# Sixteen weight low parts on VectorE and scatters alternating with scatter-adds in a one-core ViT tower kernel

## What is computed

```python
h = layernorm(einsum(layernorm(patches), W_proj) + b_proj)      # 576 tokens, 192 wide
h = h + attention(layernorm(h))                                 # 12 heads, q = cos(x) * cos(theta)
x = layernorm(h)
top_logits, top_idx = top_k(x @ router_w.T, 2)
top_w = softmax(top_logits)
for e in range(8):
    w_e = sum(top_w * (top_idx == e))
    hid = silu(x @ Wg[e].T) * (x @ Wu[e].T)
    out = out + hid @ Wd[e].T * w_e[:, None]
h = h + out
```

## Time and profile before

| What | Value |
|---|---|
| median of 3 runs | 224.12 us (221.51 to 225.14) |
| profiled execution: own time | 221.61 us |
| its span, first to last instruction | 219.8 us |
| mean granted TensorE clock | 0.959 of full speed |
| busy: TensorE, VectorE, ScalarE, GpSimd | 88%, 61%, 58%, 65% of the span |
| first expert step begins | 106.18 us |

### The profile page before, as it was taken

The page is one execution under the profiler, slowest core; times in us unless marked ns, Lnnn a source line. Parts: engine busy times, 40 slices in busy tenths (PEclk is TensorE's granted clock), DMA queues, the critical chain, the costliest instruction groups (busy, mean ns, idle before and its releaser), DMA issues.

```text
span 219.8 us, 4734 instructions
## 1 busy us (share of the span) xinstructions
PE 193.2 (88%) x1549; PEld 148.5 (68%) x1549; DVE 133.2 (61%) x418; ACT 127.7 (58%) x296; POOL 142.5 (65%) x190
## 2 busy tenths in 40 slices
PE   0599999999998879899999999995999986999950
PEld 0588999999996556473576777763676754677630
DVE  3789998369977846664733576865355441444420
ACT  0534468983598999899576667652344441344430
POOL 7699855599999724999895887785224322222222
PEclk9999999999999999976999999999699998899996
DMA  5999999689577731666676135444411223222111
GB/s 191 411 432 303 388 396 398 243 289 372 151 217 234 236 104 40 203 186 181 215 212 187 49 101 154 126 87 91 81 21 18 25 33 47 50 32 45 18 18 18
DMA packets 17152, 36.29 MB, mean 165 GB/s; under 512 B 2633, under 2 KB 7017, under 8 KB 16489
## 3 DMA queue, kind: packets, MB, share of 16 engines
q1 hardware_dynamic: 13753, 27.43, 39.1%
q0 software_dynamic: 2944, 2.76, 8.5%
q10 hardware_dynamic: 432, 5.80, 6.4%
HBM read 31.63 MB, written 4.36 MB: 164 GB/s over the span
## 4 chain that ended last, share of the span: by engine, by line
PE 59%; DMA 13%; POOL 8%; ACT 6%; issue 5%; DVE 4%; SPq 2%; POOLq 1%; ACTq 0%; DVEq 0%
PE ps L1249 19%; DMA experts<-x_t 7%; PE ps L1468 3%; PE ps L1473 3%; PE ps L1472 3%; PE ps L1470 3%; PE ps L1469 3%; PE ps L1480 3%; DMA out<-shared 3%; POOL slot_x L604 3%; PE ps L1228 2%; PE ps L1497 2%; PE ps L1496 2%; PE ps L1498 2%; ACT experts L702 2%
## 5 line engine op out<-in xcount | busy, mean ns | idle before, releaser
L413 POOL TENSOR_TENSOR experts<-stage,experts 128x528 bf16<-128x528 f32 x52 | 60.9, 1202 | 18.4 <-ACT experts L667 18.3
L1249 PE MATMUL ps<-experts 128*117 128x193 f32 (+1 forms) x320 | 55.9, 334 | 8.6 <-DVE experts L933 8.1
L1249 PEld LDWEIGHTS ps<-experts 128*117 128x117 f32 (+1 forms) x320 | 53.5, 185 | 9.5 <-DMA experts<-x_t 8.5
L1179 DVE TENSOR_TENSOR shared<-shared,ps 128x256 f32<-128x256 f32 x48 | 20.2, 421 | 46.7 <-ACT shared L834 46.7
L834 ACT ACTIVATE shared<-ps 128x256 f32<-128x256 f32 x48 | 18.5, 384 | 36.8 <-PE ps L1473 36.8
L667 ACT CAST experts<-stage 128x528 f16<-128x528 f32 x64 | 38.8, 631 | 1.0 <-DMA stage<-w_exp 1.0
L649 ACT ACTIVATE experts<-experts 128x468 f32<-128x468 f32 x40 | 22.7, 589 | 18.3 <-POOL experts L506 6.9
L618 POOL DMA_INDIRECT out<-shared x8 | 12.4, 1545 | 29.0 <-ACT shared L859 23.5
L1496 PE MATMUL ps<-experts,shared 128*128 128x192 f16 (+1 forms) x96 | 24.1, 251 | 1.6 <-DVE shared L1184 1.6
L1497 PE MATMUL ps<-experts,shared 128*128 128x192 bf16 (+1 forms) x96 | 24.1, 251 | 0.0
L1498 PE MATMUL ps<-experts,shared 128*128 128x192 f16 (+1 forms) x96 | 24.1, 251 | 0.0
(11 more groups left out here) (230 smaller groups left out, 340.3 us busy)
## 6 DMA issues: line engine op xcount, KB each, us to landing
stage<-w_exp SPq DMA_DIRECT2D x64, 264.0 KB, 3.1
experts<-x_t ACTq DMA_DIRECT2D x3, 1888.0 KB, 10.1
experts<-w_proj SPq DMA_DIRECT2D x4, 768.0 KB, 7.9
experts<-x_t SPq DMA_DIRECT2D x4, 472.0 KB, 8.6
experts<-x_t SPq DMA_DIRECT2D x1, 1888.0 KB, 15.1
slot_x<-experts SPq DMA_DIRECT2D x1, 1032.0 KB, 6.1
shared<-slot_x SPq DMA_DIRECT2D x8, 129.0 KB, 2.1
out<-h SPq DMA_DIRECT2D x1, 351.0 KB
```

The source lines that it names most:

```text
L413: ops.tensor_tensor(lo_w[:, to + EW:to + EW + PW], stage[:, n % STAGES, :], hi_w[:, to:to + PW], ALU.subtract).then_inc(split_pool if on_p ...
L1249: last = mm(dst, xbuf[:, t % 2, k, 0:m], gw[:, k, :], start=k == 0, stop=k == KT - 1)
```

## The change

Four edits. The low parts of pieces 48 to 51 go from GpSimd to VectorE, which now has sixteen, one in each of sixteen steps from 2 to 19; GpSimd has five behind the attention phase instead of nine. Scatters and add-outs alternate: two scatters, add-out 0, two scatters, add-out 1, and so on up to the tenth scatter, and then the other add-outs. ScalarE casts one piece more (46) ahead of the experts, so that every later cast comes a step earlier.

```diff
--- before.py
+++ after.py
@@ -59,7 +59,7 @@
     STAGES = 7
     GROUPS = [(0, 3), (3, 5)]
     GN = 3
-    POOL_FIRST = 52
+    POOL_FIRST = 48
     VEC_TILES = (1, 2, 4)
     EPS = 1e-5
     BIG = 512.0
@@ -73,8 +73,8 @@
-    VEC_PIECES = tuple(range(52, 64))
-    VEC_STEPS = (8, 9, 11, 12, 14, 15, 16, 17, 18, 19, 20)
+    VEC_PIECES = tuple(range(48, 64))
+    VEC_STEPS = (2, 3, 4, 5, 6, 8, 9, 11, 12, 13, 14, 15, 16, 17, 18, 19)
     def on_pool(n):
         return n not in VEC_PIECES
@@ -622,12 +622,11 @@
             pool.wait_ge(blank_out, 32)
             pool.wait_ge(xs_ready, len(GROUPS))
             pool.wait_ge(out_base, 32)
-            scatter_rows(0, 6)
-            add_out(0)
-            scatter_rows(6, 9)
-            add_out(1)
-            scatter_rows(9, 10)
-            for c in range(2, CHUNKS):
+            scatter_rows(0, 2)
+            for c in range(4):
+                add_out(c)
+                scatter_rows(2 + 2 * c, 4 + 2 * c)
+            for c in range(4, CHUNKS):
                 add_out(c)
         @block.scalar
@@ -825,7 +824,7 @@
                 last = a.activation(gexp[0:TOK, t:t + 1], top[0:TOK, t, 0:1], ACT.Exp, bias=top[0:TOK, t, 1:2], scale=-1.0)
             last.then_inc(gexp_ready, 1)
             load_table(ACT.Silu)
-            high_parts(44, 46)
+            high_parts(44, 47)
             def silu(n):
                 sc.wait_ge(gu_done, n + 1)
@@ -859,7 +858,7 @@
                 a.activation(yc[:, c % YB, :], pcol(Y_BANKS[c % 2], 0, D), ACT.Copy, scale=w).then_inc(y_ready, 1)
             rows_high(0)
-            high = 46
+            high = 47
             for n in range(NSTEP):
                 c, r = divmod(n, STEPS)
                 silu(n)
@@ -1212,9 +1211,7 @@
                 if r == 2 and 1 <= c <= E:
                     slot_facts(c - 1)
                 if n in VEC_STEPS:
-                    rests(52 + VEC_STEPS.index(n), 53 + VEC_STEPS.index(n))
-                if n == VEC_STEPS[-1]:
-                    rests(63, 64)
+                    rests(48 + VEC_STEPS.index(n), 49 + VEC_STEPS.index(n))
             hidden_low(NSTEP - 1)
         @block.tensor
```

## The result

The changed kernel takes 211.87 us (median of 4 executions, 211.42 to 212.41), the kernel before 223.56 (221.51 to 225.14, the three shown ahead of the prediction and one more). The ratio is 0.951 with a 95% interval of 0.943 to 0.958: faster. The prediction was 213.0 us in a range of 210.5 to 219.0.

The account below looks back on a forecast made before the run. TensorE was taken to bound the expert phase, losing time only in two holes: - 4.62 - 4.85 + 0.3 = - 9.2 us on the profiled 221.61 gives 212.4. Predicted 213.0 us, range 210.5 to 219.0.

Parts of the forecast that it names:

- Hole one: TensorE's 2.21 us wait before step 21 for piece 63, with slow clock behind it, goes: 4.62 us gained.
- Hole two: TensorE's 3.05 us wait in step 34 for chunk 12's rows, behind queued add-outs, goes with its slow clock: 4.85 us.
- The sum of holes: Both TensorE holes, before step 21 and in step 34, go whole in the full change: 9.47 us together.
- The last scatter: On GpSimd's alternating queue the last scatter is issued at 145.0 us, against 148.82 before.
- the slack in step 22: Chunk 8's rows arrive at 150.0 and TensorE wants them at 153.0: 3.0 us slack, so scatters stay hidden.
- rival one: Each VectorE low part costs a GpSimd scatter 0.70 us, the last slips 6.3 us, TensorE idles in step 22: 217.5 us; chance 0.12.
- Low parts against GpSimd's: VectorE's low parts in steps 2 and 3 wait 0.6 us each on GpSimd's; cost on the path 0, at most 0.2.
- Rival four: VectorE's low parts wait on GpSimd's, gate products come late, TensorE falls to 1.2 GHz: 224.9 us; chance 0.03.
- The port between VectorE and GpSimd: Nine low parts fall on scatters at 0.25 us each, 2.3 us, rather than 0.70 each, 6.3 us, by the exclusive lock.
- The cast: One more ScalarE cast ahead of the experts moves TensorE's first expert step back by 0.3 us, bounds 0 to 1.
- The signs: Among the signs of being right: each add-out from the fifth on waits for ScalarE's yield, not for a landing.
- 213.0 rather than 212.4: The sum gave 212.4 us from a fast profiled execution of 221.61; the median before was 224.12, so 213.0 was predicted.

Follow-up runs that it names:

- the run with the last two in step 20: Changed kernel with the low parts of pieces 62 and 63 both behind step 20's products, as before: 215.76 us, ratio 0.970 to the kernel before.
- The table: All eight combinations of moving pieces 48 to 51 off GpSimd, making piece 63 in step 19, and alternating the queue: ratios to the kernel before from 1.007 to 0.951.
- the old queue with relief: Changed kernel with the old order of scatters and add-outs, pieces 48 to 51 still off GpSimd: 217.11 us, second run 216.74 us (ratio 0.975).
- the two runs whose first low part on VectorE is in step 3: Pieces 48 to 51 moved to VectorE, last two low parts in step 20: with the old queue and casts 216.74 us, with alternation and extra cast 215.76 us.
- two fills: Changed kernel with two idle fills of a dead buffer on GpSimd in front of the first scatter: 213.09 us, ratio 0.955 to the kernel before.
- five fills: Changed kernel with five idle fills of a dead buffer on GpSimd in front of the first scatter: 218.35 us.

## Why the prediction was right, point by point

- **Hole one** (predicted 4.62 us, measured 4.67): the step was right. In the changed kernel piece 63's low part stands at the place where it was expected, and the run with the last two in step 20 brings the hole of 2.21 us back alone. But the 4.62 us are three things: 0.57 is the wait in step 19 (the prediction placed it in step 18), which the earlier first add-out removes and not the place of piece 63, 2.38 is the hole, and 1.67 is slow clock, which is less certain than the sum made it: in that run's profile it didn't come.
- **Hole two** (4.85 against 5.01): right, and so was its cause, the add-outs' backlog. What the prediction left open is which edit clears it. The table shows that it needs both the early start and the alternation once hole one is gone; the old queue with relief keeps 3.45 us of it.
- **The sum of holes** was right only because all causes are removed together. Taken singly, two of the three edits are worth between +0.7% and -0.7%: each takes away a hole behind which another wait was hidden. The prediction looked at what is late next for the full change alone.
- **The last scatter** (145.0 predicted, 147.35 measured) and **the slack in step 22** (3.0 us predicted, 0.2 to 0.5 measured) are the step that was mis-sized. Of the 2.35 us, 0.6 net stand ahead of the first scatter (GpSimd starts its five low parts 0.3 later, and they take 6.25 us instead of 5.75 beside VectorE's; in the two runs whose first low part on VectorE is in step 3, they took 5.78); 1.0 is in four lengthened scatters and add-outs; 0.65 in add-out 1's wait for the landing of add-out 0, which took 4.5 us to land, and 5.3 from issue to issue where the prediction used 4.18, a row from much later. The rest of the slack went to the loads: four of them issued together need up to 2.8 us until TensorE can use the first (152.44 to 155.28 with two fills), not the 2.2 of a single one. The forecast stood, but with a sixth at most of the margin that it claimed, and rival one (a queue held up, 217.5) was nearer than its 0.12: five fills, which delay the queue by other means, give 218.35. That hole two went whole was sound; that the scatters stayed hidden was in part luck.
- **Low parts against GpSimd's** (0.6 us of wait each, no cost to TensorE): 0.65 and 0.33, so right for the first, and without cost to TensorE for both. Rival four is out.
- **The port between VectorE and GpSimd**: the prediction weighed the Trainium skill (SBUF — State Buffer, "SBUF: two separate sides") against a scatter that wasn't lengthened. After the change the scatter issued at 127.58, amid VectorE's low part of 127.41 to 128.11, took 1.41 us instead of 1.0, and the one at 142.47 took 1.34; the one at 131.31 was under way when a low part began at 131.72, and took 1.02. The two low parts:

```profile
127.41 0.70 DVE L413 TENSOR_TENSOR experts<-stage,experts 128x528 bf16<-128x528 f32 x1
...
131.72 0.70 DVE L413 TENSOR_TENSOR experts<-stage,experts 128x528 bf16<-128x528 f32 x1
```

A scatter that is issued during a low part waits for the rest of it, less some 0.1 us (0.53 left and 0.41 lost at 127.58, 0.48 and 0.34 at 142.47). The row that seemed to speak against it isn't "in the middle" of the low part, as the prediction read it: at 148.82 in the trace of before, the low part had 0.13 us left. Where VectorE starts first, this agrees with the exclusive lock of the Trainium skill, which goes to whoever starts first. Where the scatter starts first it doesn't: the low part of 131.72 took its usual 0.70 us, and so did all others in the profiles that began well inside a scatter or add-out. The prediction also read the 1.25 us of the first scatter as held up by VectorE. It is 1.25 or 1.26 us in all fourteen profiles, wherever the low parts lie. The error was to read the rule as a whole low part for each scatter, 6.3 us; what is lost is the remainder only, and only for some, about 0.8 us here.
- **The cast**: 0.3 us predicted, 0.21 between the two profiles, where ScalarE reads the first chunk's rows 0.20 us later. The size is not shown beyond this pair: over all profiles the first expert step begins between 105.93 and 106.97 us with the cast and between 105.61 and 107.11 without.
- **The signs**: one of them held in part only. The sixth add-out (153.34) and the last (205.40) waited for a landing and not for a yield.
- **213.0 rather than 212.4**: the 0.6 us added for the distance between profile and median wasn't needed. The executions of before spread over 3.6 us and those after over 1.0. That fits slow clock behind holes in some executions and none without holes, but of the executions without a profile only the mean clock of the whole span is known, so it is not shown. The choice of base mattered more: the sum taken from the shown median of 224.12 would have given 214.9.

## What to carry to other kernels

When two chains feed one full engine at different points, removing the first hole alone may only lengthen the second, whose end is a time on another engine's clock; find for each hole what sets its end, and take them out together. Size a slack by the slowest rows of a kind and not by a typical one: the first add-out took 4.5 us to land here, another with two fills 5.5, where most take 3.5.

## What the runs showed of the hardware that I had not expected

- The same hole of TensorE (2.21 us, at the same place in the program) was followed by a granted clock of 0.50 in the kernel before and of 1.00 in the run with the last two low parts in step 20. A hole of 3.45 us was followed by 1.00 too. A hole's price is its length for certain, and in some executions slow clock on top: 1.5 to 2.8 us in these profiles by the lengths of the steps behind them, the most behind the holes of 3.71 and 6.47 us in step 22.
- Most of the indirect add-outs land 3.4 to 3.6 us after their issue, but single ones take up to 5.6 us, early (5.5 us for the one issued at 139.90 with two fills) and late (5.4 us at 183.30 in the second run of the old queue, 5.6 us at 179.64 without the extra cast). What holds them up was not tried.
- VectorE's low parts and GpSimd's operations hold each other up, but not alike. Among GpSimd's own low parts VectorE's waited 0.65 and 0.33 us. A scatter or add-out issued during a VectorE low part was up to 0.5 us longer, by what was left of that low part less some 0.1 us. A low part that began well inside a scatter or add-out took 0.70 us, as one does alone.
